# One turned block per item instead of three per two, a ring of sixteen gathered blocks, and the second mixture's weight blocks copied by VectorE

## The chip, the cores and the metric

The kernel runs on one core of one Trainium2 chip. The metric is the time of one execution on the device in microseconds (us), lower is better.

## The reference

The input is x of shape (8, 128, 16, 16), which is 2048 tokens of 128 channels. Four blocks follow each other, each added to its input: a linear-attention convolution block, a mixture of 8 experts (the first mixture), a self-attention block, and a mixture of 16 experts (the second). Only the two mixtures matter here:

```
# first mixture, on layer-normed tokens: 8 experts, 2 per token
top_vals, top_idx = top_k(flat @ gate_w.T, 2);  top_w = softmax(top_vals)
out = sum over chosen e of  top_w * (gelu(flat @ w1[e] + b1[e]) @ w2[e] + b2[e])     # 128 -> 512 -> 128

# second mixture: 16 experts, 2 per token
top_vals, top_idx = top_k(x @ router_w.T, 2);  weights = softmax(top_vals)
out = sum over chosen e of  weights * ((silu(x @ gate_w[e]) * (x @ up_w[e])) @ down_w[e])   # 128 -> 256 -> 128
```

## The kernel before

Everything is float32. Five engines run programs written out by hand, tied by semaphores; there is no scheduler. A mixture is worked on in blocks of 128 (token, expert) pairs sorted by expert, `NB` = 32 blocks. Since an expert's pairs end inside a block, the work goes by *items*: one block with one expert, 39 items in the first mixture (`r` = 0) and 47 in the second (`r` = 1).

What each engine does in a mixture:

- **GpSimd (POOL)**, `moe_pool`: 32 indirect DMAs, each of which gathers the 128 rows of a block from `tok_dram` into one slot of the ring `x_rows` (L534), then 32 indirect DMAs that scatter the finished blocks of `y_acc` (tile `wide`) to `y_dram` (L541). A gather into a slot that has been used waits until TensorE has turned the block that was in it (semaphore `turned`, `RING` = 8 slots). Scatter s waits until item s + E has been added up. All 64 are issued in this order from one queue.
- **TensorE (PE)**, `moe_tensor`: step n multiplies the weights of item n-1 with its block (L1452, 4 matmuls, 8 records in the trace, "the up product"), turns some blocks (L1462, a transpose from `x_rows` into bank 0 or 1), and multiplies item n-3 with its down weights (L1473, 8 records in the first mixture, 4 in the second). How many blocks are turned by the end of step n is `turned_by(n)`.
- **ScalarE (ACT)**, `moe_act`: step n copies the weight block of item n out of the big weight tile, at an address held in a register (L721, `w_block`, three slots), copies the turned blocks of the step from the bank to `x_cols` (L724), and applies gelu (L732) or silu (L738) to item n-1.
- **VectorE (DVE)**, `moe_vector`: in the first mixture it adds the bias (L1058) and adds the result up (L1081, L1086). In the second it multiplies silu with the second half of the bank (L1066, `h_cols`) and adds the result up (L1086). At step 2 it also works out masks for all items (`item_masks`, L1022 to L1025).

The waits around the change: the up product of item j waits for `w_block` of item j, for j + 1 turned and copied blocks, and for the bias or silu product of item j-2. The copy of weight block n waits for the up product of item n-3. The expert and block numbers of four items at a time are loaded to registers by `item_load` (L339). The pace of the turning is one function:

```
def turned_by(n):
    return min(NB, 1 + 3 * n // 2)
```

Row loads of the second mixture's weights on the SP queue wait for `turned` of the first mixture at 4, 8, 12 and 16.

Of the kernel before, what the change touches and what calls it, by code (L numbers as in the profile page):

```python
# [35 lines left out]
ACT = mybir.ActivationFunctionType  # L36
# [30 lines left out]
E0, F0 = 8, 512  # L67
# [1 line left out]
M0 = F0 // 128  # L69
LN_C_EPS, LN_T_EPS, BN_EPS, DIV_EPS = 1e-6, 1e-5, 1e-5, 1e-15  # L70
W1_LOADS = 4
RING = 8
LOADS = 4
EXPERT, BLOCK = 0, 1

# [1 line left out]
NB = 2 * T // 128  # L77
# [9 lines left out]

def turned_by(n):

    return min(NB, 1 + 3 * n // 2)  # L90


ATT_SCALE = float(C) ** -0.5
# [5 lines left out]
def metaformer(nc, x, w_qkv, w_dw, w_pw, w_proj, bn_gamma, bn_beta, bn_mean, bn_var,  # L99
# [10 lines left out]
    with ctx:  # L110
# [3 lines left out]
        def sem(name):  # L114
            return ctx.enter_context(nc.semaphore(name))
# [162 lines left out]
        y_in = [sem(f"y_in{c}") for c in range(NCH)]  # L278
        y_weighed, y_added, y_turned, x_moe = sem("y_weighed"), sem("y_added"), sem("y_turned"), sem("x_moe")

        class Moe:

            def __init__(m, n):
                m.gathered = [sem(f"m{n}_gathered{i}") for i in range(RING)]
                m.scattered = sem(f"m{n}_scattered")
                m.part = sem(f"m{n}_part")
                m.turned = sem(f"m{n}_turned")
                m.x_copied = sem(f"m{n}_x_copied")
                m.w = sem(f"m{n}_w")
                m.up = sem(f"m{n}_up")  # L290
                m.h_in = sem(f"m{n}_h_in")
                m.act = sem(f"m{n}_act")
                m.down = sem(f"m{n}_down")
                m.y = sem(f"m{n}_y")
# [149 lines left out]
        def _(pool):  # L444
# [79 lines left out]
            def moe_pool(r, E):  # L524
# [6 lines left out]
                for j in range(NB):  # L531
                    if j >= RING:
                        pool.wait_ge(m.turned, j - RING + 1)
                    pool.indirect_dma_start(  # L534
                        out=x_rows[:, j % RING, :], out_offset=None, in_=tok_dram[r],
                        in_offset=bass.IndirectOffsetOnAxis(ap=token[r][:, j:j + 1], axis=0))\
                        .then_inc(m.gathered[j % RING], 16)
                pool.wait_ge(rt_table, 4 * r + 2)
                for s in range(NB):
                    pool.wait_ge(m.y, s + E)  # L540
# [10 lines left out]
        def _(act):  # L551
# [153 lines left out]
            def moe_act(r, E, NI):  # L705
                m = moe[r]
                if r == 0:
                    act.wait_ge(moe_w[0], 48)
                    act.wait_ge(rt_table, 3)
                else:  # L710
                    act.wait_ge(moe_w[1], 16 * 3 * W1_LOADS)
                    act.wait_ge(rt_table, 7)
                load_table((ACT.Gelu_apprx_tanh, ACT.Silu)[r])
                for n in range(NI + 1):
                    if n < NI:
                        if n % LOADS == 0:
                            es = item_load(act, mybir.EngineType.Activation, r, EXPERT, n, NI, E - 1)
                        e = es[n % LOADS]
                        if n >= 3:
                            act.wait_ge(m.up, n - 2)  # L720
                        act.activation(w_block[:, n % 3, :], (w_up0, w_up1)[r][:, bass.ds(e * F0, F0)], ACT.Copy).then_inc(m.w, 1)  # L721
                    for k in range(turned_by(n - 1) if n else 0, turned_by(n)):
                        act.wait_ge(m.turned, k + 1)
                        act.activation(x_cols[:, k * 128:(k + 1) * 128], bank[k % 2][:, 0:128], ACT.Copy)\  # L724
# [68 lines left out]
        def _(dve):  # L793
# [241 lines left out]
            def moe_vector(r, E, NI, w_up):  # L1035
# [6 lines left out]
                for n in range(NI + 3):  # L1042
# [4 lines left out]
                    if n < NI:  # L1047
                        j = n
                        if j % LOADS == 0:
                            for i, v in enumerate(item_load(dve, mybir.EngineType.DVE, r, EXPERT, j, NI, E - 1)):  # L1050
                                e[j + i] = v
                    if 0 <= n - 1 < NI:
                        j = n - 1
                        if r == 0:
# [91 lines left out]
        def _(pe):  # L1146
# [286 lines left out]
            def moe_tensor(r, E, NI, w_down):  # L1433
# [7 lines left out]
                for n in range(NI + 3):  # L1441
# [14 lines left out]
                        mm.then_inc(m.up, 1)  # L1456
                        at.pop(j)
                    for k in range(turned_by(n - 1) if n else 0, turned_by(n)):
                        pe.wait_ge(m.gathered[k % RING], 16 * (k // RING) + 16)
                        if k >= 2:  # L1460
                            pe.wait_ge(m.x_copied, k - 1)
                        pe.transpose(bank[k % 2][:, 0:128], x_rows[:, k % RING, :], ident[:, :]).then_inc(m.turned, 1)  # L1462
# [125 lines left out]
```

## Time and profile before

| | us |
|---|---|
| median of 3 runs | 469.87 (469.56 to 471.03) |
| profiled execution | 473.52 |
| its span, first to last instruction | 471.8 |
| first mixture, from its first gather to its last scatter | 157.6 to 265.5 in the span |
| second mixture, the same | 349.1 to 454.1 in the span |

TensorE is busy for 376.3 us of the span, VectorE for 234.2, ScalarE for 213.5, GpSimd for 196.1. In the trace an engine's row has its start in us from the span's start, its duration, and in brackets how long the engine had been idle before it and what ended that. Matmuls overlap in the pipeline, so the starts of rows tell the pace better than their durations. "issue" is idle time that no wait explains, and "remote" in the rows is a release that the profile can't attribute.

### The profile page before, as it was taken

How to read it: one execution, taken by the hardware profiler on the slowest of the kernel's cores; microseconds unless marked ns; L12 is line 12 of the kernel's file. 1: busy time of each engine (PE TensorE's matmuls, PEld its weight loads, DVE VectorE, ACT ScalarE, POOL GpSimd, SP SyncE). 2: the span in 40 equal slices, each digit the busy share in tenths (PEclk: the TensorE clock that was granted, in tenths of full speed). 3: DMA queues.
4: the chain of work that ended last, by engine and by line, in shares of the span. 5: the costliest groups of instructions: out<-in, count | busy, mean ns of one | idle time of the engine just before them, and what ended most of it. 6: DMA issues, size and time to landing. Idle time of an engine off the chain costs nothing.

```text
span 471.8 us, 7850 instructions
## 1 busy us (share of the span) xinstructions
PE 376.3 (80%) x2497; PEld 316.2 (67%) x2497; DVE 234.2 (50%) x547; ACT 213.5 (45%) x549; POOL 196.1 (42%) x209
## 2 busy tenths in 40 slices
PE   6999999999574758985999399898466778878813
PEld 4667999998352548974999255675335767878812
DVE  2559665633347415643677284475752333434415
ACT  3256223333437425643566173473642455655403
POOL 9419993430002555665455300000237454555630
PEclk9599999999997677996899787999857799999965
DMA  5014446433653265911011340000031111111136
GB/s 146 0 21 81 101 92 90 69 44 40 214 149 102 61 179 167 305 48 46 23 41 35 101 107 0 1 0 1 18 88 52 34 42 37 36 41 40 40 109 186
DMA packets 44014, 35.26 MB, mean 75 GB/s; under 512 B 3800, under 2 KB 39752, under 8 KB 43976
## 3 DMA queue, kind: packets, MB, share of 16 engines
q1 hardware_dynamic: 36412, 24.70, 20.2%
q0 software_dynamic: 4096, 8.40, 6.0%
q10 hardware_dynamic: 3468, 1.67, 2.2%
q8 instruction: 22, 0.36, 0.3%
q14 instruction: 16, 0.13, 0.1%
HBM read 21.12 MB, written 7.34 MB: 60 GB/s over the span
## 4 chain that ended last, share of the span: by engine, by line
PE 68%; DVE 8%; issue 6%; ACT 6%; DMA 5%; another core or an unknown queue 3%; ACTq 1%; SPq 1%; POOL 1%; POOLq 0%; DVEq 0%
PE bank L1452 18%; PE bank L1473 12%; PE bank L1363 10%; PE bank L1214 2%; DMA ln_sq<-y 2%; PE bank L1462 2%; PE bank L1313 2%; PE bank L1499 2%; ACT w_block L721 2%; PE bank L1397 2%; PE bank L1232 2%; PE bank L1298 2%; PE bank L1540 1%; PE bank L1239 1%
## 5 line engine op out<-in xcount | busy, mean ns | idle before, releaser
L1452 PE MATMUL bank<-x_cols,w_block 128*128 x688 | 103.2, 298 | 23.1 <-ACT w_block L721 8.9
L1452 PEld LDWEIGHTS bank<-x_cols,w_block 128*128 128x128 f32 x688 | 92.5, 209 | 29.3 <-issue 29.1
L534 POOL DMA_INDIRECT x_rows<-tok,token x64 | 61.4, 960 | 66.1 <-DVE dest L1004 28.6
L541 POOL DMA_INDIRECT y<-wide,dest x64 | 62.3, 974 | 51.7 <-DVE wide L1086 41.3
L1473 PE MATMUL bank<-w_down,h_cols 128*128 x500 | 73.9, 286 | 2.7 <-DVE wide L1086 1.8
L1473 PEld LDWEIGHTS bank<-w_down,h_cols 128*128 128x128 f32 x500 | 66.0, 201 | 4.0 <-issue 3.7
L1363 PE MATMUL bank<-cmap,cw 128*128 128x112 f32 (+2 forms) x480 | 57.5, 275 | 0.0
L1363 PEld LDWEIGHTS bank<-cmap,cw 128*128 128x128 f32 x480 | 55.8, 192 | 1.5 <-issue 1.4
L721 ACT ACTIVATE w_block<-w_up 128x512 f32 x86 | 53.6, 624 | 1.1 <-issue 0.6
L324 POOL TENSOR_TENSOR cw<-pw_in,dw_band 128x640 f32<-128x640 f32 x24 | 39.3, 1661 | 32.0 <-ACT pw_in L606 17.0
L528 POOL MEMSET wide<- 128x4096 f32 x2 | 7.0, 3512 | 106.9 <-DVE xs L1137 64.3
L1066 DVE TENSOR_TENSOR h_cols<-h_in,bank 128x256 f32<-128x256 f32 x47 | 19.8, 421 | 62.3 <-PE bank L1473 37.8
L732 ACT ACTIVATE h_cols<-h_in 128x512 f32<-128x512 f32 x39 | 24.6, 630 | 34.8 <-PE bank L1473 23.2
L1058 DVE TENSOR_TENSOR h_in<-bank,wT 128x512 f32<-128x512 f32 x39 | 27.0, 691 | 23.6 <-PE bank L1452 8.0
L724 ACT ACTIVATE x_cols<-bank 128x128 f32<-128x128 f32 x64 | 15.6, 273 | 44.3 <-remote 21.6
L324 DVE TENSOR_TENSOR cw<-pw_in,dw_band 128x640 f32<-128x640 f32 x24 | 28.4, 1205 | 3.2 <-PE bank L1363 2.8
L1462 PE MATMUL bank<-ident,x_rows 128*128 128x128 f32 x64 | 16.8, 312 | 12.7 <-ACT x_cols L724 6.1
L738 ACT ACTIVATE h_in<-bank 128x256 f32<-128x256 f32 x47 | 18.1, 386 | 18.9 <-PE bank L1452 17.5
L1081 DVE TENSOR_TENSOR y_part<-bank,b_all 128x128 f32<-128x128 f32 x39 | 11.3, 290 | 23.7 <-PE bank L1473 17.7
L1152 PE MATMUL bank<-ones,ident 128*128 128x512 f32 x22 | 15.6, 845 | 7.4 <-DMA ln_sq<-y 7.4
L747 ACT ACTIVATE wide<-wide,pair_w 128x128 f32<-128x128 f32 x32 | 10.2, 390 | 24.9 <-DMA ln_sq<-y 24.9
L1462 PEld LDWEIGHTS bank<-ident,x_rows 128*128 128x128 f32 x64 | 9.8, 162 | 16.7 <-issue 16.7
(213 smaller groups left out, 583.6 us busy)
## 6 DMA issues: line engine op xcount, KB each, us to landing
cmap<-heads SPq DMA_DIRECT2D x48, 64.0 KB
w_up<-in_L_ffn_w_dram SPq DMA_DIRECT2D x1, 2048.0 KB, 8.6
tok<-ln_sq SPq DMA_DIRECT2D x8, 256.0 KB, 2.4
w_up<-in_L_ffn_gate_w_dram SPq DMA_DIRECT2D x4, 512.0 KB
w_up<-in_L_ffn_up_w_dram SPq DMA_DIRECT2D x4, 512.0 KB
w_down<-in_L_ffn_down_w_dram SPq DMA_DIRECT2D x4, 512.0 KB
wide<-y SPq DMA_DIRECT2D x8, 256.0 KB, 4.6
ln_sq<-y SPq DMA_DIRECT2D x8, 256.0 KB, 5.2
```

The source lines that it names most:

```text
L324: engine.tensor_tensor(cw[:, u % CWR, i, :, :].rearrange("p k (o x) -> p k o x", x=HW), pw_in[:, :, g].unsqueeze(1).unsqueeze(3).broadcast ...
L534: pool.indirect_dma_start(out=x_rows[:, j % RING, :], out_offset=None, in_=tok_dram[r], in_offset=bass.IndirectOffsetOnAxis(ap=token[r][:, ...
L541: pool.indirect_dma_start(out=y_dram[r], in_=y_acc[:, s * C:(s + 1) * C], in_offset=None, out_offset=bass.IndirectOffsetOnAxis(ap=dest[r][ ...
L721: act.activation(w_block[:, n % 3, :], (w_up0, w_up1)[r][:, bass.ds(e * F0, F0)], ACT.Copy).then_inc(m.w, 1)
L732: act.activation(h_cols[:, j % 2, :], h_in[:, j % 2, :], ACT.Gelu_apprx_tanh)\
L738: act.activation(h_in[:, j % 2, 0:F1], bank[2 + j % 2][:, 0:F1], ACT.Silu)\
L1058: dve.tensor_tensor(h_in[:, j % 2, :].rearrange("p (k s) -> p k s", k=M0), bank[2 + j % 2][:, :].rearrange("p (k s) -> p k s", k=M0), wT[: ...
L1066: dve.tensor_tensor(h_cols[:, j % 2, 0:F1], h_in[:, j % 2, 0:F1], bank[2 + j % 2][:, F1:2 * F1], ALU.mult).then_inc(m.h_in, 1)
L1363: mm = pe.matmul(bank[b][:, i * 128 + y0 * B:i * 128 + y1 * B], cw[:, u % CWR, i, k, :], cmap[:, t, v * GU + i, (y0 + k - EDGE) * B:(y1 + ...
L1452: mm = pe.matmul(bank[2 + j % 2][:, i * 128:(i + 1) * 128], w_block[:, j % 3, i * 128:(i + 1) * 128], x_cols[:, bass.ds(at[j], 128)], star ...
L1462: pe.transpose(bank[k % 2][:, 0:128], x_rows[:, k % RING, :], ident[:, :]).then_inc(m.turned, 1)
L1473: mm = pe.matmul(bank[6 + j % 2][:, 0:C], h_cols[:, j % 2, i * 128:(i + 1) * 128], w_down[:, bass.ds(ej * (K * C) + i * C, C)], start=(i = ...
```

## The change

Three edits. `turned_by(n)` becomes `1 + 9 * n // 8`: one block is turned in a step, and two at steps 8, 16 and 24, so the last block is turned at step 28 and not at step 21. `RING` becomes 16, so GpSimd issues 16 gathers before the first wait; its semaphores are now shared by both mixtures and counted on. And in the second mixture the weight block is copied by VectorE at the head of its step n, ahead of the multiplication of item n-1; ScalarE there only copies turned blocks and applies silu.

```diff
-RING = 8
+RING = 16
 def turned_by(n):
-    return min(NB, 1 + 3 * n // 2)
+    return min(NB, 1 + 9 * n // 8)
+        gathered = [sem(f"gathered{i}") for i in range(RING)]
         class Moe:
-                m.gathered = [sem(f"m{n}_gathered{i}") for i in range(RING)]
...
             def moe_act(r, E, NI):
                 if r == 0:
                     act.wait_ge(moe_w[0], 48)
                     act.wait_ge(rt_table, 3)
-                else:
-                    act.wait_ge(moe_w[1], 16 * 3 * W1_LOADS)
-                    act.wait_ge(rt_table, 7)
...
-                    if n < NI:
+                    if r == 0 and n < NI:
...
-                        act.activation(w_block[:, n % 3, :], (w_up0, w_up1)[r][:, bass.ds(e * F0, F0)], ACT.Copy).then_inc(m.w, 1)
+                        act.activation(w_block[:, n % 3, :], w_up0[:, bass.ds(e * F0, F0)], ACT.Copy).then_inc(m.w, 1)
...
             def moe_vector(r, E, NI, w_up):
...
+                        if j >= 3 and r == 1:
+                            dve.wait_ge(m.up, j - 2)
+                        if r == 1:
+                            dve.tensor_copy(w_block[:, j % 3, :], w_up[:, bass.ds(e[j] * UP, UP)]).then_inc(m.w, 1)
...
             def moe_tensor(r, E, NI, w_down):
-                        pe.wait_ge(m.gathered[k % RING], 16 * (k // RING) + 16)
+                        pe.wait_ge(gathered[k % RING], 16 * ((r * NB + k) // RING) + 16)
```

How it moves instructions on VectorE, in the steps of the second mixture. Before, a step is the multiplication with silu and the addition to `wide`; ISA rows set an address from a register:

```order
L1066 TENSOR_TENSOR h_cols<-h_in,bank 128x256
L339 TENSOR_LOAD items
L1086 ISA
L1086 SCALAR_TENSOR_TENSOR wide<-bank,item,wide 128x128
L1066 TENSOR_TENSOR h_cols<-h_in,bank 128x256
L1086 ISA
L1086 SCALAR_TENSOR_TENSOR wide<-bank,item,wide 128x128
```

The same place in the changed program (its L1068 and L1088 are L1066 and L1086 before):

```order
L1068 TENSOR_TENSOR h_cols<-h_in,bank 128x256
L340 TENSOR_LOAD items
L1088 ISA
L1088 SCALAR_TENSOR_TENSOR wide<-bank,item,wide 128x128
L340 TENSOR_LOAD items
L1053 ISA
L1053 COPY w_block<-w_up 128x512
L1068 TENSOR_TENSOR h_cols<-h_in,bank 128x256
L1088 ISA
L1088 SCALAR_TENSOR_TENSOR wide<-bank,item,wide 128x128
L1053 ISA
L1053 COPY w_block<-w_up 128x512
```

The copy of a later item's weights now stands between one item's addition and the next item's multiplication, with an address step of its own.

TensorE at the start of the second mixture, before:

```order
L1452 MATMUL bank<-x_cols,w_block 128x128 x4
L1462 MATMUL bank<-ident,x_rows 128x128 x2
L1452 ISA
L1452 MATMUL bank<-x_cols,w_block 128x128 x4
L1462 MATMUL bank<-ident,x_rows 128x128
L339 TENSOR_LOAD items
L1473 ISA
L1473 MATMUL bank<-w_down,h_cols 128x128
```

and the same steps after (L1454, L1464 and L1475 are L1452, L1462 and L1473 before):

```order
L1454 MATMUL bank<-x_cols,w_block 128x128 x4
L1464 MATMUL bank<-ident,x_rows 128x128
L1454 ISA
L1454 MATMUL bank<-x_cols,w_block 128x128 x4
L1464 MATMUL bank<-ident,x_rows 128x128
L340 TENSOR_LOAD items
L1475 ISA
L1475 MATMUL bank<-w_down,h_cols 128x128
```

The pair of turned blocks (x2) behind the second up product is a single one: the block that the very next up product reads.

## Rows read from the trace of the kernel before

**Rows 1.** The page: chain of waits by line, and the group of the gathers
```profile
PE bank L1452 18%; PE bank L1473 12%; PE bank L1363 10%; PE bank L1214 2%; DMA ln_sq<-y 2%; PE bank L1462 2%; PE bank L1313 2%; PE bank L1499 2%; ACT w_block L721 2%; PE bank L1397 2%; PE bank L1232 2%; PE bank L1298 2%; PE bank L1540 1%; PE bank L1239 1%
...
L534 POOL DMA_INDIRECT x_rows<-tok,token x64 | 61.4, 960 | 66.1 <-DVE dest L1004 28.6
```

**Rows 2.** Timeline, second mixture, GpSimd (start, duration, operation, idle time before it)
```profile
392.09 0.95 POOL L534 DMA_INDIRECT x_rows<-tok,token  x1 [1.14 <-remote]
...
393.34 0.95 POOL L534 DMA_INDIRECT x_rows<-tok,token  x1 [0.30 <-issue]
...
396.73 0.95 POOL L534 DMA_INDIRECT x_rows<-tok,token  x1 [1.19 <-remote]
```

**Rows 3.** By stretches: length, TensorE's up products, its weight loads, clock, DMA
```profile
184.00:208.00 24.00, 10.79 (x81) 9.55 (x80) 1.00 0.70 202
208.00:228.00 20.00, 7.22 (x41) 6.59 (x42) 0.74 0.12 37
...
380.00:398.00 18.00, 8.23 (x63) 7.37 (x62) 1.00 0.16 43
398.00:452.00 54.00, 32.68 (x240) 29.05 (x240) 1.00 0.12 38
```

**Rows 4.** The same stretches, gathers alone: length, GpSimd busy, clock, DMA
```profile
184.00:208.00 24.00, 14.40 (x16) 1.00 0.70 202
...
380.00:398.00 18.00, 10.89 (x12) 1.00 0.16 43
```

**Rows 5.** Timeline, TensorE alone, first mixture: two items in a row
```profile
238.63 1.06 PE L1452 MATMUL bank<-x_cols,w_block 128*128 x8
...
240.42 1.06 PE L1452 MATMUL bank<-x_cols,w_block 128*128 x8
```

**Rows 6.** Timeline, second mixture, TensorE and ScalarE
```profile
389.68 0.38 PE L1462 MATMUL bank<-ident,x_rows 128*128 128x128 f32 x2
...
391.86 0.45 ACT L724 ACTIVATE x_cols<-bank 128x128 f32<-128x128 f32 x2 [2.39 <-remote]
...
417.04 1.15 PE L1452 MATMUL bank<-x_cols,w_block 128*128 x8 [1.54 <-ACT w_block L721]
```

**Rows 7.** Timeline, second mixture, its first up product
```profile
352.86 2.07 PE L1452 MATMUL bank<-x_cols,w_block 128*128 x8 [0.56 <-ACT x_cols L724]
```

**Rows 8.** Groups of VectorE elsewhere, from one SBUF tile to another
```profile
L1127 DVE TENSOR_SCALAR sq_pn<-sq_p,sq_st 128x256 f32<-128x256 f32 x16 | 4.9, 351 | 0.3
...
L909 DVE TENSOR_SCALAR xs<-xs,bn 128x2048 f32<-128x2048 f32 x1 | 1.3, 1285 | 0.0
...
L889 DVE COPY tok_w<-center 128x128 f32<-128x128 f32 x2 | 2.1, 1107 | 0.0
```

**Rows 9.** Groups of instructions by line, second mixture
```profile
L721 ACT ACTIVATE w_block<-w_up 128x512 f32 x47 | 29.7, 632 | 0.9 <-issue 0.6
...
L1066 DVE TENSOR_TENSOR h_cols<-h_in,bank 128x256 f32<-128x256 f32 x47 | 19.8, 421 | 62.3 <-PE bank L1473 37.8 <-ACT h_in L738 9.9 <-remote 8.4
L738 ACT ACTIVATE h_in<-bank 128x256 f32<-128x256 f32 x47 | 18.1, 386 | 18.9 <-PE bank L1452 17.5 <-DVE h_cols L1066 1.0 <-issue 0.4
L1086 DVE SCALAR_TENSOR_TENSOR wide<-bank,item,wide 128x128 f32 x47 | 16.3, 347 | 2.9 <-issue 1.7 <-PE bank L1473 0.7
```

**Rows 10.** Waits, second mixture: in total, times, longest
```profile
PE bank L1452 <- DVE h_cols L1066: 5.5, 7, 1.3
```

**Rows 11.** Timeline, second mixture: VectorE's masks beside a gather
```profile
356.20 0.24 DVE L1022 TENSOR_SCALAR item<-item,col_id 128x47 f32<-128x47 f32 x1
356.48 0.90 DVE L1023 TENSOR_TENSOR beyond<-ends,item 128x705 f32<-128x705 f32 x1
356.70 1.49 POOL L534 DMA_INDIRECT x_rows<-tok,token  x1 [0.30 <-issue]
...
358.33 0.21 DVE L1025 TENSOR_TENSOR item<-item 128x47 f32<-128x47 f32 x1
```

**Rows 12.** Timeline, first mixture, GpSimd: the last of eight scatters in a row
```profile
217.25 0.97 POOL L541 DMA_INDIRECT y<-wide,dest  x1 [0.31 <-issue]
```

More of the change, by code:

```diff
@@ L536, in moe_pool @@
                         in_offset=bass.IndirectOffsetOnAxis(ap=token[r][:, j:j + 1], axis=0))\
-                        .then_inc(m.gathered[j % RING], 16)
+                        .then_inc(gathered[j % RING], 16)
                 pool.wait_ge(rt_table, 4 * r + 2)
```

## The prediction

> **What bounds the kernel now.** I read the page first. Its chain of waits goes over TensorE for most of its length, the up and down products of the mixtures alone for 18% and 12% [rows 1]. But each of GpSimd's 64 indirect DMAs in a mixture is nearly 1 us [rows 1], with at least 0.30 us between two of them [rows 2]: 64 x 1.26 = 81 us of the mixture's 105 or so. Next I took busy time by stretches, to see which of the two holds which stretch.
>
> First mixture, 184 to 208: 81 records, 10.1 items in 24 us, 2.37 us per item at full clock [rows 3], and 16 gathers, 1.50 us each [rows 4]. TensorE alone needs 1.79 us for an item [rows 5]. Second mixture, 380 to 398: 63 records, 7.9 items, 2.28 us per item [rows 3], and 12 gathers, again 1.50 us each [rows 4]. The ratio is the turning's three for two: 1.5 x 1.50 = 2.25. So **the gathers set the pace there, through the turning**, which asks for blocks ahead of need. The timeline shows the loop. Two blocks are turned at 389.68, ScalarE copies them only at 391.86 [rows 6], and GpSimd goes on at 392.09 after 1.14 us of idling; the next such pause is three gathers and 4.64 us later [rows 2]. Both engines wait for TensorE's count of turned blocks and get it some 1.8 us late. The profile names no cause ("remote"), and I have none. Behind the gathers, from 398 on, an item takes 54 x 8 / 240 = 1.8 us at most, some 1.7 up to the last up product [rows 3], though TensorE's work there is half of 1.79 for the up product and a quarter for the down product, 0.90 + 0.45. There the stops are again late releases, like the 1.54 us before the up product at 417.04 [rows 6].
>
> **The change part by part.** The sum is made against the profiled execution, 473.52 us; the median of the runs is 3.65 lower, and I take that off at the end.
>
> *Turning 9 for 8.* In a gather-paced stretch an item then asks for 1.125 gathers, 1.125 x 1.50 = 1.69 us. First mixture: TensorE's 1.79 plus 1.125 turnings of 0.11 (two take 0.38, one 0.27 [rows 6]) is 1.91 us and becomes the bound: 2.37 - 1.91 = 0.46 us for 10 items, **-4.6 us**. Second: TensorE has 0.90 + 0.45 + 0.12, the gathers 1.69: 2.28 - 1.69 = 0.59 for 8 items, **-4.7 us**. No turning is saved. Eleven or so move behind the stretch, but the items there that carry them are at 1.7 us with TensorE at 1.47, so they fit.
>
> Its cost: for the first 8 items a block is turned only in the step before the product that reads it. From the end of a turning over ScalarE's copy to the product TensorE idles 0.56 us with nothing between [rows 7]. The down product between covers 0.90 us in the first mixture and 0.45 in the second: 8 x 0.1, **+0.8 us**. SP's loads of the next weights, which wait for turned blocks 4 to 16, go out a few steps later, some 150 us before they are read: nothing.
>
> *Ring of 16.* GpSimd issues 16 gathers with no wait, and a later one waits for a block turned 16 before, rarely the last release at 9 for 8. I count nothing of its own, since the gain above takes gathers at today's 1.50 us; unbroken they would be 1.25 (a rival below). The scatters queued behind can be issued earlier but wait for items. The shared semaphores add no instruction.
>
> *VectorE copies the second mixture's weights.* No row shows this copy. Nearest below are 351 ns for 256 elements and 1285 for 2048; the line between them, 0.521 ns per element, gives 484 ns for 512. Above are 1107 ns for only 128 elements, where GpSimd ran all the while [rows 8], which with 384 x 0.521 more makes 1.31 us. I take **0.48**, the same access with GpSimd quiet, and keep 0.35 and 1.31. ScalarE is relieved of 632 ns per item [rows 9], which is off the path. VectorE's step was 0.42 + 0.35 [rows 9] and becomes 1.25, with the address steps some 1.4 to 1.5, as much as TensorE's 1.47. Before, block n+1 was copied right behind silu of n-1: 0.39 + 0.63 = 1.0 us after the up product of n-1 [rows 9]. Now it stands behind silu, multiplication and addition: 0.39 + 0.42 + 0.35 + 0.48 = 1.64, and TensorE wants it after 0.45 + 0.90 + 0.45 = 1.8 us. A late release that ScalarE absorbed now stops TensorE. TensorE's stops for the product with silu in the second mixture are 7 [rows 10], and 417.04 is one more: 8, each longer by one copy, 8 x 0.48 = **+3.8 us** (8 x 0.35 = 2.8 or, if all is absorbed, 0; 8 x 1.31 = 10.5 at most). Once, block 2 also waits behind the masks, which end at 358.5 [rows 11], just when its up product is due: a copy and two releases, **+0.9 us**.
>
> The Trainium skill (VectorE: DVE Perf Modes, "The TRN2 errata") gives 58 cycles plus half the elements for such a copy, which at its 0.96 GHz is an estimate of 0.33 us; the sum would be 1.2 us lower by it. The trace's 351 ns for half the size speak against it.
>
> Sum: -4.6 - 4.7 + 0.8 + 3.8 + 0.9 = **-3.8 us**: 469.7 for such an execution, **466.1 us** for the median.
>
> **The rivals.**
>
> *A, the late releases go too.* If they come from GpSimd and TensorE waiting on each other by way of eight slots, sixteen slots remove them. For: they recur every three gathers [rows 2]. Against: they go on behind 398, where no gather is left [rows 6]. Then an item costs 1.5 and not 1.7 us for the second mixture's last 29, 5.8 us more, and in the first some 5.5 of the 20 us that 208 to 228 takes for 5 items [rows 3] are saved: -3.8 - 11.3 = -15.1, **454.8 us**.
>
> *B, slower: VectorE's copy and GpSimd's DMAs hold each other.* The gather at 356.70 took 1.49 us, not 0.95, beside a VectorE operation of 0.90 us with two SBUF inputs [rows 11], and VectorE's copies of 128 elements took 1107 ns beside GpSimd's work [rows 8]. Against it: the operation at 356.20 took 0.24 us beside a gather [rows 11]. The price: 47 copies each hold an indirect DMA for 0.48 us, 22.6 us on a queue with 81 us of work in 105, of which some 16 vanish in its pauses, +6.6; and the second mixture's gain of 4.7 is gone. -4.6 + 0.8 + 3.8 + 0.9 + 6.6 = +7.5, **477.4 us**. It decides once an indirect DMA of the second mixture takes over 1.2 us on average. The Trainium skill (SBUF — State Buffer, "Who interferes with whom") has it as a rule: a float32 copy on VectorE from SBUF to SBUF takes the port pair it shares with GpSimd, and whichever comes second is blocked for the whole instruction. By that rule this rival would be sure; the trace agrees at 356.70 and not at 356.20.
>
> *C, slower: an unbroken run of DMAs holds TensorE's releases back.* The worst stretch, 208 to 228 with 3.9 us per item [rows 3], has eight scatters from 208.17 on without a pause [rows 12]. With sixteen slots both mixtures would have 32 gathers in a row, 40 us: 10 items instead of 13, some 6 us lost in each; the gains are gone; some 3 us come back, since fewer scatters are left to run in a row later. +9, **478.9 us**.
>
> *D, nothing measurable:* the pauses only move, within 1.4 us.
>
> **How the numbers follow.** About 0.3%, 1.4 us, is what a measurement can tell from no change. The forecast gets 0.42 (its own range 461 to 472: 0.33 faster, 0.07 same, 0.02 slower), A 0.15 faster, B 0.25 (0.02 faster, 0.01 same, 0.22 slower), C 0.13 slower, D 0.05 same. Together: faster 0.50, same 0.13, slower 0.37. The range leaves out half of A and the far ends of B and C: 456 to 481. The ends of the copy's price, 3.8 less and 6.7 more on the sum, lie inside it.
>
> **What would show it.** Right: up products stand 1.9 us apart at 184 to 208 and 1.7 at 380 to 398; the gathers end sooner; VectorE's copy is 0.48 us; TensorE's stops in the second mixture end with VectorE's copy. Wrong: copies over 0.7 us or indirect DMAs over 1.2 us (B); 3 to 4 us per item while the gathers run (C); no late release any more (A); or a pace that stays at 2.3 us per item, for then the turning was not what asked for it.

## The result: slower, 1.014 of the time before

The changed kernel takes 475.83 us (median of 4 runs, 474.59 to 478.07), the kernel before in the same comparison 469.72 (4 runs, 467.62 to 471.03): ratio 1.014, 95% interval 1.008 to 1.020. The forecast was 466.1 us and faster. The profiled execution is one of 474.74 us with a span of 473.0. A ratio with an interval, here and below, compares the fast runs of each kernel, those within 1.5% of its fastest; where many runs of the kernel before fall outside, the ratio of the medians of all runs stands beside it.

The page of the changed kernel: chain of waits by engine, then groups of instructions by line (operation, out<-in, count | busy us, mean ns | idle before it, what ended most of that).

```profile
PE 66%; issue 9%; DVE 9%; another core or an unknown queue 5%; DMA 5%; ACT 3%; ACTq 1%; POOL 1%; DVEq 1%; SPq 0%; POOLq 0%
...
L1454 PE MATMUL bank<-x_cols,w_block 128*128 x688 | 100.9, 293 | 43.0 <-issue 26.1
...
L535 POOL DMA_INDIRECT x_rows<-tok,token x64 | 61.4, 960 | 67.8 <-DVE dest L1002 28.7
L542 POOL DMA_INDIRECT y<-wide,dest x64 | 63.1, 985 | 56.6 <-DVE wide L1088 48.1
...
L1053 DVE COPY w_block<-w_up 128x512 f32 x47 | 20.6, 441 | 3.6 <-issue 2.5
```

and the up products on the page of before:

```profile
L1452 PE MATMUL bank<-x_cols,w_block 128*128 x688 | 103.2, 298 | 23.1 <-ACT w_block L721 8.9
```

TensorE has as many up products as before, but waits 43.0 us ahead of them and not 23.1. The gathers still take 960 ns each [rows 1]. VectorE's copy, which no row could show ahead, is 0.44 us.

By stretches, TensorE's up products (8 records an item; columns: stretch, length, busy and records, weight loads, granted clock, DMA share, GB/s). The first and the fourth stretch lie in front of those of [rows 3]; in the kernel before they were:

```profile
157.00:184.00 27.00, 10.50 (x50) 9.39 (x51) 0.72 0.44 131
349.00:380.00 31.00, 14.68 (x76) 13.21 (x77) 0.71 0.16 42
```

and in the changed kernel all six are:

```profile
157.00:184.00 27.00, 5.53 (x32) 4.68 (x32) 0.75 0.36 107
184.00:208.00 24.00, 12.73 (x88) 11.51 (x88) 0.92 0.59 174
208.00:228.00 20.00, 7.64 (x52) 7.14 (x53) 0.83 0.32 102
349.00:380.00 31.00, 10.06 (x50) 8.92 (x51) 0.76 0.16 45
380.00:398.00 18.00, 11.64 (x81) 10.01 (x79) 0.94 0.13 37
398.00:452.00 54.00, 34.39 (x248) 30.04 (x248) 1.00 0.12 37
```

The stretches of [rows 3] have gained, 88 records for 81, 52 for 41, 81 for 63. What was won there is lost ahead of them: from 157 to 184 TensorE starts 4 items in 27 us where it started 6, from 349 to 380 6 in 31 where it started 9 to 10. By 228 both kernels have started 172 records of the first mixture. The gathers of those two stretches:

```profile
157.00:184.00 27.00, 17.91 (x19) 0.75 0.36 107
...
349.00:380.00 31.00, 20.20 (x21) 0.76 0.16 45
```

They run without a pause, where [rows 4] had 1.50 us for each. The timeline at the end of the first mixture's run, GpSimd (start, duration, operation, idle time before it and what ended it):

```profile
176.96 0.94 POOL L535 DMA_INDIRECT x_rows<-tok,token  x1 [0.30 <-issue]
178.21 0.94 POOL L535 DMA_INDIRECT x_rows<-tok,token  x1 [0.30 <-issue]
179.46 0.94 POOL L535 DMA_INDIRECT x_rows<-tok,token  x1 [0.30 <-issue]
184.08 0.94 POOL L535 DMA_INDIRECT x_rows<-tok,token  x1 [3.68 <-remote]
```

TensorE at the same time:

```profile
169.41 2.07 PE L1454 MATMUL bank<-x_cols,w_block 128*128 x8 [4.49 <-issue]
171.28 0.42 PE L1464 MATMUL bank<-ident,x_rows 128*128 128x128 f32 x1
171.49 1.91 PE L1475 MATMUL bank<-w_down,h_cols 128*128 x8
184.31 2.07 PE L1454 MATMUL bank<-x_cols,w_block 128*128 x8 [10.91 <-issue]
```

And the two engines that TensorE was waiting for:

```profile
180.98 0.63 ACT L730 ACTIVATE h_cols<-h_in 128x512 f32<-128x512 f32 x1 [11.76 <-remote]
181.52 0.61 ACT L719 ACTIVATE w_block<-w_up 128x512 f32 x1
183.84 0.28 ACT L722 ACTIVATE x_cols<-bank 128x128 f32<-128x128 f32 x1 [1.71 <-remote]
```

```profile
181.04 0.29 DVE L1083 TENSOR_TENSOR y_part<-bank,b_all 128x128 f32<-128x128 f32 x1 [12.69 <-remote]
```

Read them together. TensorE's last product is over at 173.40. VectorE's addition of its result starts at 181.04, and ScalarE copies the block turned at 171.28 only at 183.84; its gelu ahead of that had itself waited 11.76 us. Neither engine has other work meanwhile. GpSimd has issued its last gather of the run at 179.46. So **TensorE's completions reach the others late while the gathers run, and the last of them only after the run's end**, and TensorE, which needs their results for its next items, stands for 10.91 us. The same is in the second mixture: ScalarE's copy at 364.92, amid the run, waited 6.80 us ("remote"), and the one at 376.22, 3.2 us behind the end of the last of 21 gathers, 10.74. The granted clock is 0.75 in the mean from 157 to 184, but it was 0.72 in the kernel before, so it is no part of the difference. The up product at 184.31 takes 2.07 us, as at the lower level (1.2 GHz), not 1.06, and the one at 169.41 ahead of the stop did too.

From the first gather to the last scatter the first mixture went from 106.9 us to 109.6, the second from 104.0 to 108.7. The rest of the span is 6.1 us shorter. Two profiled executions of the changed kernel (this one and e5) differ by 4.7 us in span, so parts of that size in one profile aren't explained one by one.

### The profile page after: what moved, and what is told of

It reads as the page before. It is cut to its first block, busy times and chain, and to the rows that moved or that the text cites. A ratio compares the mean times of both kernels' runs of the same rounds, so it can differ in the third digit from the quotient of the medians.

```text
span 473.0 us, 7847 instructions
## 1 busy us (share of the span) xinstructions
PE 367.2 (78%) x2497; PEld 311.6 (66%) x2497; DVE 252.4 (53%) x594; ACT 188.4 (40%) x502; POOL 197.0 (42%) x209
## 4 chain that ended last, share of the span: by engine, by line
PE 66%; issue 9%; DVE 9%; another core or an unknown queue 5%; DMA 5%; ACT 3%; ACTq 1%; POOL 1%; DVEq 1%; SPq 0%; POOLq 0%
PE bank L1454 16%; PE bank L1365 10%; PE bank L1475 10%; PE bank L1315 2%; PE bank L1216 2%; PE bank L1464 2%; PE bank L1399 2%; DMA ln_sq<-y 2%; PE bank L1300 1%; PE bank L1501 1%; PE bank L1542 1%; PE bank L1234 1%; PE bank L1222 1%; PE bank L1241 1%
## 5 line engine op out<-in xcount | busy, mean ns | idle before, releaser
L1454 PE MATMUL bank<-x_cols,w_block 128*128 x688 | 100.9, 293 | 43.0 <-issue 26.1
L1454 PEld LDWEIGHTS bank<-x_cols,w_block 128*128 128x128 f32 x688 | 89.4, 203 | 49.2 <-issue 48.2
L1475 PE MATMUL bank<-w_down,h_cols 128*128 x500 | 74.8, 289 | 1.7 <-DVE wide L1088 1.7
L1475 PEld LDWEIGHTS bank<-w_down,h_cols 128*128 128x128 f32 x500 | 67.5, 205 | 2.3 <-issue 2.0
L722 ACT ACTIVATE x_cols<-bank 128x128 f32<-128x128 f32 x64 | 16.8, 272 | 73.8 <-PE bank L1464 38.7
L1068 DVE TENSOR_TENSOR h_cols<-h_in,bank 128x256 f32<-128x256 f32 x47 | 19.7, 420 | 45.5 <-issue 17.3
L736 ACT ACTIVATE h_in<-bank 128x256 f32<-128x256 f32 x47 | 17.9, 382 | 24.7 <-PE bank L1454 23.1
L719 ACT ACTIVATE w_block<-w_up 128x512 f32 x39 | 24.0, 615 | 0.2 <-PE bank L1454 0.2
L1053 DVE COPY w_block<-w_up 128x512 f32 x47 | 20.6, 441 | 3.6 <-issue 2.5
L1464 PE MATMUL bank<-ident,x_rows 128*128 128x128 f32 x64 | 17.7, 292 | 5.1 <-ACT x_cols L722 3.6
```

Source lines behind the costliest of these rows:

```text
L719: act.activation(w_block[:, n % 3, :], w_up0[:, bass.ds(e * F0, F0)], ACT.Copy).then_inc(m.w, 1)
L1053: dve.tensor_copy(w_block[:, j % 3, :], w_up[:, bass.ds(e[j] * UP, UP)]).then_inc(m.w, 1)
L1068: dve.tensor_tensor(h_cols[:, j % 2, 0:F1], h_in[:, j % 2, 0:F1], bank[2 + j % 2][:, F1:2 * F1], ALU.mult).then_inc(m.h_in, 1)
L1454: mm = pe.matmul(bank[2 + j % 2][:, i * 128:(i + 1) * 128], w_block[:, j % 3, i * 128:(i + 1) * 128], x_cols[:, bass.ds(at[j], 128)], star ...
L1475: mm = pe.matmul(bank[6 + j % 2][:, 0:C], h_cols[:, j % 2, i * 128:(i + 1) * 128], w_down[:, bass.ds(ej * (K * C) + i * C, C)], start=(i = ...
```

## The experiments

The chips that ran these kernels are of two kinds: in the result and on two of the chips of the experiments the kernel before takes about 470 us, on three others 428 to 430. A ratio below is always to the kernel before on the same chip, in the same comparison, with its 95% interval; behind it stands the ratio of the medians of all runs. "The 470 chips" and "the 430 chips" name the kinds. The first four expectations were written for the chip of the result, and met a 430 chip.

### Undoing parts of the change

The changed kernel with the ring of before:

```diff
-RING = 16
+RING = 8
```

> The changed kernel with the ring back at 8. Theory R (an unbroken run of GpSimd's gathers holds back TensorE's completions, and sixteen slots are what lets the run go to 20 gathers): the first run of gathers ends at 12 as before, the stop of 11 us in the first mixture (171.5 to 184.3) and of 8 us in the second (368.5 to 376.7) shrink to the 3 to 4 us of before, and the time is 463 to 468 us. Rival P (VectorE's copies are the loss): still 474 to 477 us.

The changed kernel with ScalarE's copies in both mixtures:

```diff
-                    if r == 0 and n < NI:
+                    if n < NI:
...
-                            dve.tensor_copy(w_block[:, j % 3, :], w_up[:, bass.ds(e[j] * UP, UP)]).then_inc(m.w, 1)
```

> Turning 9 for 8 and the ring of 16, but ScalarE copies the weight blocks of the second mixture as before. Theory R: the long stops stay in both mixtures, 473 to 476 us, within 3 us of the changed kernel. Rival P (VectorE's copies hold GpSimd's DMAs, or are late themselves): 466 to 469 us.

Of the kernel before, only the turning changed, then only the ring:

```diff
-    return min(NB, 1 + 3 * n // 2)
+    return min(NB, 1 + 9 * n // 8)
```

> The kernel before with the turning at 9 for 8 alone, ring of 8. By the sum of the prediction (4.6 + 4.7 us gained, 0.8 lost): 461 to 464 us. Rival T (the turning ahead of need costs nothing, since late releases set the pace whatever it is): 468 to 471 us.

```diff
-RING = 8
+RING = 16
```

> The kernel before with the ring at 16 alone, turning 3 for 2. Theory R: a first run of about 20 gathers, long stops of 8 us and more at the start of both mixtures, 473 to 480 us. If slots were only missing (rival A of the prediction): under 465 us.

Only the copies moved to VectorE:

> Only VectorE's copies of the change: turning by 3 for 2 and a ring of 8 as before. Q: after the blocks are turned, the same 1.44 to 1.55 us an item with 0.45 more in every fourth, against 1.34 before: with some 27 items after the turning 5 to 6 us, and while it turns 3 blocks for 2 items TensorE's item is 1.6 us, so that the loop of 1.55 costs only its fourth steps, 1 to 2 us more: ratio 1.015 to 1.02. F: the copies cost most while gathers run, little afterwards: ratio 1.005 to 1.01. Rival C of the prediction (runs of gathers hold TensorE back) has no part in it: by C alone ratio 1.00.

And on 470 chips once more the changed kernel, and the three versions with ScalarE's copies:

> The changed kernel as it is, to place it on this chip beside the others. Theory Q (queue): VectorE's copy of item n+1 stands in its queue behind the multiplication of item n-1 and the addition of item n-3, so that up product, SiLU, multiplication, addition, copy, up product form a loop; in e1_ring8 it was 1.06 us of up product + 2.05 us from its end to the up product two items on, 1.55 us an item where TensorE's own work is 1.45 (while it turns) or 1.34 (afterwards), and every fourth step, with its register loads, 0.45 us more. By it the second mixture lasts about 9 us longer than with ScalarE's copies, and this kernel is 1.010 to 1.015 of the one before. Theory F (a fuller VectorE and GpSimd's indirect DMAs hold each other): the same time, so this run alone does not tell them apart; by F the gathers or the copies would show longer than 1.2 or 0.6 us in the mean. If this chip holds TensorE's releases back during unbroken runs of gathers (as in the profile of the changed kernel), ratio 1.014, else nearer 1.012.

> The changed kernel with ScalarE copying in both mixtures (turning 9 for 8, ring of 16), as e2_scalar_copies. Theory H (TensorE's releases held back): on a chip where the kernel before takes about 470 us, TensorE's completions reach the others late while GpSimd issues indirect DMAs one behind another, so that a longer unbroken run of gathers costs; a ring of 16 lets 20 gathers run where a ring of 8 with 3 for 2 let 13, 7 x 1.25 = 8.75 us more in each mixture, of which about half is lost: ratio 1.015 to 1.025 with a wait of over 8 us on TensorE in each mixture, whoever copies. Theory Q (the loop through VectorE's copy) alone: 0.985 to 0.992, as on the chip where the kernel before takes 430 us. On such a chip both expect 0.985 to 0.992, since nothing is held there.

> Only turning 9 for 8 (ring 8, ScalarE copies), as e3_turn_only. H on a chip of 470 us: the ring stops the gathers as before, runs of 12 or 13, so ratio 0.99 to 1.00; on a chip of 430 us 0.993 to 1.00. If turning 9 for 8 is itself what lengthens the runs, 1.01 or more on a chip of 470 us.

> Only the ring of 16 (turning 3 for 2, ScalarE copies), as e4_ring16_only. H on a chip of 470 us: runs of 20 gathers or more, ratio 1.015 to 1.025 by the ring alone. On a chip of 430 us 0.985 to 0.995.

Measured:

| kernel | turning | ring | copies | on a 430 chip | on a 470 chip |
|---|---|---|---|---|---|
| changed (e14, e5) | 9/8 | 16 | VectorE | 1.018 (1.012 to 1.023), all 1.015 | 1.022 (1.016 to 1.028), all 1.021 |
| e1 | 9/8 | 8 | VectorE | 1.019 (1.011 to 1.027), all 1.018 | |
| e2, e9 | 9/8 | 16 | ScalarE | 0.988 (0.981 to 0.995), all 0.990 | 1.027 (1.019 to 1.035), all 1.012 |
| e3, e10 | 9/8 | 8 | ScalarE | 0.996 (0.991 to 1.002), all 0.992 | 1.012 (1.002 to 1.022), all 1.005 |
| e4, e11 | 3/2 | 16 | ScalarE | 0.989 (0.980 to 0.998), all 0.996 | 1.018 (1.010 to 1.026), all 1.007 |
| e7 | 3/2 | 8 | VectorE | | 1.001 (0.997 to 1.006), all 1.001 |

E9 to e12 ran on one chip, where the kernel before took from 463.05 to 474.72 us, and the medians of all runs make their ratios lower by 0.7 to 1.4%. So e9 is slower by either measure, and the sizes of e10, e11 and e12 are not certain.

The two columns differ. **On a 430 chip the copies are the loss**: e1 against e3 is 438.13 - 426.94 = 11.2 us, and the changed kernel is some 3% over e2, on another chip, while turning and ring together gain about 1%. **On a 470 chip ring and turning are the loss** (e9), and the copies alone cost nothing that shows: e7 lies between -0.3% and +0.6%. Whether they cost something on top of ring and turning stays open, since e9 (1.027, all 1.012) and the changed kernel (1.022, all 1.021) ran on two chips. Theory H (runs of GpSimd's indirect DMAs hold back TensorE's completions) was right on e9 and, by the ratio with the interval, on e11. It was wrong on e10, for which it expected 0.99 to 1.00. Theory Q (VectorE's copy closes a loop over the engines) expected 1.015 to 1.02 for e7 and failed on that chip.

### What the two kinds of chip do differently

The changed kernel on a 430 chip, GpSimd and TensorE in the first mixture's run of gathers:

```profile
171.12 0.94 POOL L535 DMA_INDIRECT x_rows<-tok,token  x1 [0.30 <-issue]
172.37 1.02 POOL L535 DMA_INDIRECT x_rows<-tok,token  x1 [0.30 <-issue]
173.69 0.95 POOL L535 DMA_INDIRECT x_rows<-tok,token  x1 [0.30 <-issue]
```

```profile
171.47 1.06 PE L1454 MATMUL bank<-x_cols,w_block 128*128 x8
172.36 0.27 PE L1464 MATMUL bank<-ident,x_rows 128*128 128x128 f32 x1
172.47 1.06 PE L1475 MATMUL bank<-w_down,h_cols 128*128 x8
173.36 1.06 PE L1454 MATMUL bank<-x_cols,w_block 128*128 x8
```

The gathers are as long and as dense as on the chip of the result. TensorE goes on beside them, an item every 1.89 us. All 32 gathers run in a row there, and 20 scatters behind them.

Counted from the timelines: the runs of at least 5 indirect DMAs in a row (starts at most 1.55 us apart) and the items whose up product starts from the first DMA's start to 1.25 us behind the last's; then a mixture's length, first gather to last scatter.

| 470 chips | runs in the first mixture: DMAs / items | length | second mixture | length |
|---|---|---|---|---|
| before | 12 / 4, 9 / 3 | 106.9 | 7 / 2, 6 / 1 | 104.0 |
| changed | 20 / 4, 7 / 3 | 109.6 | 21 / 5 | 108.7 |
| changed again (e5) | 20 / 4, 7 / 3 | 111.7 | 21 / 5 | 110.8 |
| e9, ring 16, 9/8 | 20 / 4, 7 / 3 | 108.7 | 20 / 4 | 107.7 |
| e11, ring 16 alone | 21 / 4, none later | 104.7 | 21 / 6 | 108.9 |
| e10, 9/8 alone | 11 / 3, 15 / 4 | 110.4 | 7 / 2, 5 / 2, 7 / 3 | 101.5 |
| e7, copies alone | 12 / 4, 9 / 3 | 106.5 | 13 / 5, 5 / 2 | 105.6 |
| e8, changed, copy before the addition | 20 / 4, 7 / 3 | 110.1 | 20 / 4 | 110.5 |
| e6, changed, copy ahead | 20 / 4, 7 / 3 | 110.0 | 6 / 3, 15 / 2 | 109.7 |

However long a run of 11 or more is, TensorE gets 2 to 6 items into it: 12 DMAs (15 us) let 4 pass, 20 (25 us) let 4 pass. (E6's run of 15 begins 1.76 us behind one of 6.) The longest run does not by itself give a mixture's length: e11's first mixture has a run of 21, none later, and is no longer than that of the kernel before (104.7 us against 106.9). On a 430 chip the changed kernel has a run of 52 DMAs with 31 items. A ring of 16 makes the first run 8 DMAs longer, 10 us. E10 shows the other end: with a ring of 8 and turning 9 for 8 the last gather comes later, the scatters that are ready meanwhile go out in one run of 15 with that gather, and TensorE stands then, as this row of e10 says of ScalarE amid that run:

```profile
224.13 0.63 ACT L732 ACTIVATE h_cols<-h_in 128x512 f32<-128x512 f32 x1 [5.45 <-remote]
```

So the ring lengthens the stop at the gathers, and the later gathers move one to the scatters. That the runs hold TensorE is read from these timelines and from the ring of 4 below; by what means they do, and why the chips differ, isn't known.

### A ring of 4

The changed kernel with a ring of 4, and the copy ahead (its diff stands below):

> The changed kernel with a ring of 4 and VectorE's copy one item further ahead (e6_copy_ahead with RING 4). H on a chip of 470 us: runs of some 6 to 8 gathers, TensorE's longest wait in a mixture under 5 us, ratio 0.98 to 1.00, at least 2% under e6_copy_ahead's 1.018. If it is not the length of the run that holds TensorE but each gather, nothing is gained and the ratio stays near 1.02. On a chip of 430 us: Q expects 0.985 to 1.0 (the copy is out of the loop; a ring of 4 makes gathers wait for the turning at 1.3 us a block), F (a fuller VectorE) 1.01 or more.

It met a 470 chip: 1.014 (1.006 to 1.023), by the medians of all runs 1.004, against 1.018 for the same kernel with a ring of 16 on another. Of three parts of the expectation the first holds: the first runs have 6 DMAs, and from the first up product to the 24th it is 52 us, where the kernel before takes 70. That is the strongest sign that the run's length is what costs. The others fail. The first mixture is 111.6 us long, since 19 DMAs, 17 of them scatters, run in a row behind the last gathers. VectorE and GpSimd there:

```profile
238.10 0.97 POOL L542 DMA_INDIRECT y<-wide,dest  x1 [0.31 <-issue]
```

```profile
241.36 0.69 DVE L1061 TENSOR_TENSOR h_in<-bank,wT 128x512 f32<-128x512 f32 x1 [11.11 <-remote]
```

VectorE waited 11.11 us for an up product and got it 2.3 us behind the end of the last scatter of the run. So TensorE's completions come late in runs of scatters as in those of gathers.

### The copy's place in VectorE's queue

VectorE copies one item further ahead; three buffers, 47 copies, nothing else changed:

```diff
-                    if n < NI:
-                        j = n
+                    for j in ([n] if r == 0 else [0, 1] if n == 0 else [n + 1]):
+                        if j >= NI:
+                            continue
```

> The changed kernel with VectorE copying one item further ahead: in the step in which it multiplied item n-1 it copies n+1, not n, with three buffers as they are; as many copies, of the same length, on the same engine. Theory Q: the copy leaves the loop, the up products of the second mixture stand 1.45 us apart while blocks are turned and 1.34 afterwards, no wait on a copy but the first, ratio 0.985 to 0.992 of the kernel before, some 2.3% under e5. Theory F (VectorE is too full, or holds GpSimd): VectorE does as much in as little time, so no gain, ratio as e5 (1.010 to 1.015).

> The changed kernel with VectorE's copy one item further ahead, as e6_copy_ahead. On a chip where the kernel before takes about 430 us theory Q (the copy closes a loop in VectorE's queue) expects up products 1.45 us apart while blocks are turned and 1.34 after, ratio 0.985 to 0.992 of the kernel before, and over 1.5% under e14; theory F (a fuller VectorE) expects no difference from e14. On a chip of 470 us: as before, 1.018, under e14 by no more than 0.5%.

> The changed kernel as it is. On a chip of 430 us Q expects 1.01 to 1.02 (e1_ring8 had 1.019); on a chip of 470 us 1.014 to 1.022 as before.

On a 470 chip 1.018 (1.012 to 1.024) for it beside 1.022 for the changed kernel: no difference that can be told, where Q had expected 0.985 to 0.992. On a 430 chip **0.984 (0.975 to 0.992) beside 1.018 (1.012 to 1.023)**, 423.59 us against 434.30. One item of lead is worth 10.7 us there, and the changed kernel's loss becomes a gain. The gain is less certain than the lead: the kernel before has a median of 427.73 us over all its runs on that chip, which makes 0.990 and 1.015. The changed kernel on that chip, VectorE:

```profile
357.53 0.42 DVE L1068 TENSOR_TENSOR h_cols<-h_in,bank 128x256 f32<-128x256 f32 x1 [0.94 <-ACT h_in L736]
357.87 0.34 DVE L1088 SCALAR_TENSOR_TENSOR wide<-bank,item,wide 128x128 f32 x1
358.13 0.42 DVE L1053 COPY w_block<-w_up 128x512 f32 x1
358.98 0.42 DVE L1068 TENSOR_TENSOR h_cols<-h_in,bank 128x256 f32<-128x256 f32 x1 [0.43 <-ACT h_in L736]
359.32 0.34 DVE L1088 SCALAR_TENSOR_TENSOR wide<-bank,item,wide 128x128 f32 x1
359.58 0.58 DVE L1053 COPY w_block<-w_up 128x512 f32 x1
```

and TensorE's up products:

```profile
355.65 1.15 PE L1454 MATMUL bank<-x_cols,w_block 128*128 x8 [0.31 <-DVE w_block L1053]
...
357.20 1.06 PE L1454 MATMUL bank<-x_cols,w_block 128*128 x8
...
358.69 1.15 PE L1454 MATMUL bank<-x_cols,w_block 128*128 x8
...
360.30 0.93 PE L1454 MATMUL bank<-x_cols,w_block 128*128 x6
```

The loop: up product at 357.20, ScalarE's silu from 358.57 to 358.95, multiplication at 358.98, addition, copy from 359.58 to 360.16, up product at 360.30. Two items in 3.10 us, 1.55 each, where TensorE has work for 1.45. The step before 355.65, with the register loads of four items' addresses on VectorE, took 2.03. Neither the multiplication nor the addition is needed by the product that waits; they only stand ahead of the copy. With the copy ahead VectorE's multiplication of 358.13 and the addition are followed, at 358.73, by a copy that TensorE needs an item later, and TensorE never stops:

```profile
356.34 1.06 PE L1455 MATMUL bank<-x_cols,w_block 128*128 x8
...
357.79 1.06 PE L1455 MATMUL bank<-x_cols,w_block 128*128 x8
...
359.24 1.06 PE L1455 MATMUL bank<-x_cols,w_block 128*128 x8
```

In the same 26 us, TensorE's up products without and with the lead (columns as above):

```profile
340.00:366.00 26.00, 17.46 (x127) 15.22 (x127) 1.00 0.21 53
```

```profile
340.00:366.00 26.00, 18.82 (x144) 17.52 (x144) 1.00 0.20 52
```

VectorE has the same work in both kernels, and in this stretch it is even busier with the lead (18.71 us against 16.83). Theory F, that a fuller VectorE or one that GpSimd blocks is the cause, falls on that chip. With the lead the second mixture is 81.6 us long (87.7 without), which is GpSimd's 64 x 1.27 us in one run of 64 DMAs: the next bound there.

> The changed kernel with the copy of item n+1 moved over one instruction in VectorE's queue, ahead of the addition of item n-3 and still behind the multiplication of item n-1 (the register loads come ahead of that multiplication). Q: the loop loses the addition's 0.26 us, 3.11 to 2.85 us for two items, 1.43 an item: just under the 1.45 of the turning, over the 1.34 afterwards: ratio between e6 and e5, 0.992 to 1.003, up products 1.45 apart while blocks are turned and 1.43 afterwards. F: as e5.

```diff
+                    if r == 1 and 0 < n < NI - 1:
+                        j = n + 1
+                        if j >= 3:
+                            dve.wait_ge(m.up, j - 2)
+                        dve.tensor_copy(w_block[:, j % 3, :], w_up[:, bass.ds(e[j] * UP, UP)]).then_inc(m.w, 1)
```

This one met only a 470 chip, where the copies' place made no difference (e6), and gave 1.022 (1.016 to 1.029), as the changed kernel: it decides nothing.

### Breaking the runs

Two kernels were to show by their time that unbroken runs hold TensorE. The first pauses GpSimd after every second gather:

```diff
+                    if j % 2 == 1:
+                        pool.memset(pause[:, :], 0.0).then_inc(m.paused, 1)
+                        pool.wait_ge(m.paused, j // 2 + 1)
```

> The changed kernel with a pause of GpSimd (a memset of about 1 us into a buffer of its own, waited for) after every second gather: 32 pauses, some 38 us more of GpSimd's time, no less work for anybody. Theory H (TensorE's completions are held back while indirect DMAs run unbroken, until about 2 us after the last) on a chip of 470 us: no wait of TensorE over 5 us while gathers run, 9 items or more in the first 25 us after the first gather instead of 4, ratio 1.5% or more under e14's in spite of the added work, unless the scatters, which are then later and run unbroken at the end, take it back. If the long waits have another cause (ScalarE, the blocks' arrival), the pauses only add to them, ratio over 1.03. On a chip of 430 us, where nothing is held and GpSimd's DMAs run unbroken through the mixtures, the pauses cost: ratio 1.02 to 1.06.

> As e15_pause (1.048 on a chip of 430 us): the changed kernel with a pause of GpSimd after every second gather. Theory H on a chip of 470 us (e5_changed_again 1.022 there): no wait of TensorE over 5 us while gathers run, 9 items or more in the first 25 us after the first gather instead of 4 or 5; the later scatters may take back what is won, so the time may be 1.00 to 1.03, under the 1.048 that the same pauses cost where nothing is held. If the waits have another cause they stay at 11 us and the ratio is over 1.05. On a chip of 430 us: 1.048 again.

The second, with the copy ahead and a ring of 8, lets a gather wait for the turning five blocks back and issues scatters between the later gathers:

```diff
-                    if j >= RING:
-                        pool.wait_ge(m.turned, j - RING + 1)
+                    if j >= 5:
+                        pool.wait_ge(m.turned, j - 4)
...
+                    if j < NB - 1 and turned_by(done + E + 3) + 2 <= j:
+                        scatter(done)
+                        done += 1
```

> The changed kernel with the copy ahead (as e13), a ring of 8 of which a gather uses 5 (it waits for the turning five blocks back), and the scatters issued between the later gathers as their blocks are done instead of all after the last gather. H on a chip of 470 us: runs of at most 8 DMAs, no burst of scatters behind the last gather, TensorE's longest wait under 4 us, ratio 0.97 to 1.0. If what holds TensorE is the sum of GpSimd's DMAs and not their unbroken runs, ratio 1.01 or more. On a chip of 430 us the 64 DMAs of 1.27 us are 81 us of the mixture whatever their order: 0.98 to 1.0.

> As e16_interleaved (1.015 on a chip of 430 us): copy ahead, gathers that wait for the turning five blocks back, scatters between the later gathers. H on a chip of 470 us: no run of over 10 DMAs, no wait of TensorE over 4 us, ratio 0.97 to 1.0. If the sum of GpSimd's DMAs holds TensorE and not their unbroken runs, 1.01 or more. On a chip of 430 us 1.015 again.

Both met 430 chips both times, where nothing is held: 1.048 (1.040 to 1.057) and 1.054 (1.047 to 1.061) for the pauses, as expected, 1.015 (1.005 to 1.025; all 1.029) and 1.033 (1.027 to 1.040) for the other order, where e16 expected 0.98 to 1.0 and e18 1.015. They show only that such a cure costs 2 to 6% on a 430 chip. The pauses also lengthen VectorE's copies, 0.54 us in the mean and not 0.44; the one at 358.86 in e15, beside GpSimd's memset of 0.96 us, takes 1.44. On a 470 chip neither was tried, so the direct test of theory H is missing.

## Why the prediction was wrong

The measured 475.83 us lies inside the prediction's widest range, 456 to 481, but on the slower side, to which it gave 0.37; the forecast, 466.1 us and faster, failed.

**Turning 9 for 8, -4.6 and -4.7 us, with the ring of 16 of which "I count nothing of its own".** This is the step that failed on the chip of the result: the sum put at nothing what sixteen slots do to the run of gathers. Its pace was right where it applied: two items of the changed kernel in the stretch of [rows 3], 1.89 us apart where 1.91 was worked out.

```profile
187.92 1.06 PE L1454 MATMUL bank<-x_cols,w_block 128*128 x8
...
189.81 1.06 PE L1454 MATMUL bank<-x_cols,w_block 128*128 x8
```

But the stretch begins only as the run of gathers ends, and the ring makes that run 20 or 21 gathers long where it was 12 or 13. In place of -4.6 us the first mixture shows +2.7; in place of +0.8 (-4.7, and +0.8 for turning just in time, +3.8 and +0.9 for the copies) the second shows +4.7. Ring alone is 1.018, turning alone 1.012, both without the copies 1.027; by the medians of all runs 1.007, 1.005 and 1.012.

**VectorE's copies, +3.8 and +0.9 us.** On that kind of chip the term was too large where it was measured alone: 1.001 for the copies alone, from -1.5 to +2.6 us. The stops are there, TensorE idles 16.4 us ahead of the second mixture's up products in e7 and 12.4 before, but the mixture is only 1.6 us longer (105.6 against 104.0), less than profiles of one kernel differ. The copies' own length, 0.44 us, was forecast well as 0.48. The wait behind the masks was there once:

```profile
355.25 1.00 PE L1454 MATMUL bank<-x_cols,w_block 128*128 x3 [2.18 <-DVE w_block L1053]
```

On a 430 chip the 3.8 was too small by a factor of three: 11.2 us between e1 and e3. The prediction had the pieces: VectorE's step "1.4 to 1.5, as much as TensorE's 1.47" and a copy at 1.64 us behind an up product where TensorE wants it after 1.8. It added the bare durations and left out what lies between two engines: in the rows of e14 silu starts 0.31 us behind the up product and the next up product 0.14 us behind the copy, and every fourth step has the register loads. 1.64 became 2.04 us, and a slack of 0.16 became a stop of 0.2 every two items.

**Rival C, 0.13, 478.9 us.** This is nearest to what happened, and its mark, "3 to 4 us per item while the gathers run", was passed: 27 us for 4 items. That its time is within 3.1 us of the measured one is luck, for its numbers were off in both directions. Its +9 leaves out the 5.5 us of costs that the forecast counts (0.8, 3.8 and 0.9). The run was 20 gathers, not 32, since a stopped TensorE turns no blocks; and TensorE lost far more in it than 3 items of 13. Much of that comes back later, at 1.9 us an item where it was 2.37. The prediction had seen both halves of it, the 3.9 us per item beside eight scatters [rows 12] and completions that come 1.8 us late for no cause the profile names [rows 6], and gave it 0.13. The kernel before shows it on a second look: its first 12 gathers run unbroken too, with 4 items beside them.

**Rival B, 0.25.** It falls. The indirect DMAs of the changed kernel's second mixture take 0.99 us in the mean, far from 1.2. One beside a copy takes somewhat more: on the 430 chip the gather at 356.31 starts 0.13 us behind the copy of 356.18 (0.42 us) and takes 1.10 us where most take 0.94; the longest of the result's second mixture, the scatter at 432.19 beside the copy of 432.14, takes 1.22. The Trainium skill (SBUF — State Buffer, "Who interferes with whom") would have the one that comes second blocked for the whole of the other, which leaves 0.29 us for the gather and 0.37 for the scatter; the rows show 0.16 and 0.25.

**Rival A** is the 430 chip, in effect: no release that the profile marks "remote" in either mixture, and the ring of 16 alone gives 0.989 there (0.996 by the medians). It was no matter of the kernel.

The estimate of 0.33 us for the copy by the Trainium skill (VectorE: DVE Perf Modes, "The TRN2 errata") is 0.11 under the 0.44 measured. The same section says of that row of its table that it under-predicts single operations, which the prediction left out; the trace agrees with that.

## What to carry to other kernels

Before letting a queue run further ahead, look at what else happens while it runs unbroken. Here, on one kind of chip, TensorE got no more items into a run of 20 of GpSimd's indirect DMAs than into one of 12, and the timelines of before held the sign: count the other engines' work within each run. When a step of a pipeline is moved to another engine, draw the loop it joins, instruction by instruction in queue order, with the 0.1 to 0.3 us between engines; if it closes within two items, issue it one item earlier, which here was worth 10.7 us on one kind of chip for no work at all. A small gain measured on one chip may be a loss on another: ring and turning with ScalarE's copies gave 0.988 on one kind and 1.027 on the other, and no version that met both kinds beats the kernel before on both.

## What was not expected of the hardware

The same program, the kernel before, takes 470 us on some chips and 428 to 430 on others, though a gather of the changed kernel takes as long on both (0.96 and 0.97 us). The difference is where GpSimd's indirect DMAs run: the changed kernel's mixtures are 109.6 and 108.7 us long on the one, 85.7 and 87.7 on the other. On the slower kind, other engines see TensorE's completions some 12 us late at the worst in the result's profile, in a run of gathers (the block turned at 171.28, copied at 183.84), and late in runs of scatters too (11.11 us of waiting in e12); on the other no wait of any engine in the mixtures is marked "remote" (e1 to e4, e13, e14). What makes the completions late no trace here shows.
